# Six PSUM banks for the first propagation of batch 0, and a reordered start, in a two-layer graph kernel

## The reference

```python
h = relu(layernorm(x))                       # (8, 1024, 256)
Xw = h @ Wv + bv;  sj = Xw @ aw[:d];  si = Xw @ aw[d:]
e = leaky_relu(sj[:, None, :] + si[:, :, None] + ab, 0.2)
T = adj * exp(e);  T = T / (T.sum(-1) + 1e-12)
H = h @ Wk[0] + T @ (h @ Wk[1]) + T @ T @ (h @ Wk[2]) + bk.sum(0)   # as the kernel groups it
x = x + relu(H)
h = relu(layernorm(x));  A1 = adj + I;  dh = rsqrt(A1.sum(-1))
x = x + relu(dh * (A1 @ (dh * h)) @ kernel + bias)
```

## Time and profile before

| | us |
|---|---|
| median of 3 runs | 764.09 |
| the runs | 763.99, 764.09, 766.89 |
| profiled execution | 765.5 |
| its span (first to last instruction) | 763.7 |
| PE busy, share of the span | 749.1, 98% |
| DVE busy | 623.8, 82% |
| ACT busy | 536.9, 70% |
| POOL busy | 187.1, 24% |
| moved by DMA | 143.32 MB, mean 188 GB/s |

### The profile page before, as it was taken

The page is one execution under the profiler, slowest core; times in us unless marked ns, Lnnn a source line. Parts: engine busy times, 40 slices in busy tenths (PEclk is TensorE's granted clock), DMA queues, the critical chain, the costliest instruction groups (busy, mean ns, idle before and its releaser), DMA issues.

```text
span 763.7 us, 14034 instructions
## 1 busy us (share of the span) xinstructions
PE 749.1 (98%) x5099; PEld 689.8 (90%) x5099; DVE 623.8 (82%) x1417; ACT 536.9 (70%) x1044; POOL 187.1 (24%) x190
## 2 busy tenths in 40 slices
PE   8879999999999999999999999999999999999997
PEld 8778998999889898998979999899998999889986
DVE  7877888978888789887998879897888877986665
ACT  3887796667966689557885678856696677956451
POOL 3023141222403224041321304122140222402330
PEclk9989999999999999999999999999999999999999
DMA  6557348753486445872657625776248654455511
GB/s 223 211 183 251 115 163 277 224 203 129 156 284 210 174 153 172 284 248 85 194 186 266 231 77 189 241 258 223 95 155 275 214 208 139 156 184 183 168 64 55
DMA packets 63909, 143.32 MB, mean 188 GB/s; under 512 B 6768, under 2 KB 32864, under 8 KB 63840
## 3 DMA queue, kind: packets, MB, share of 16 engines
q1 hardware_dynamic: 55072, 111.75, 43.9%
q10 hardware_dynamic: 8768, 30.68, 11.4%
HBM read 133.96 MB, written 8.45 MB: 186 GB/s over the span
## 4 chain that ended last, share of the span: by engine, by line
PE 94%; DVE 3%; ACT 1%; issue 1%; DMA 0%; POOL 0%; POOLq 0%; DVEq 0%; ACTq 0%
PE acc L1176 15%; PE acc L1178 15%; PE acc L1177 15%; PE da L1044 14%; PE db L1044 8%; PE da L1142 4%; PE tp L1142 4%; PE da L1144 4%; PE da L1143 4%; PE tp L1144 4%; PE tp L1143 4%; PE acc L1076 1%; PE acc L1195 1%; DVE t_raw L806 1%; PE acc L1197 1%
## 5 line engine op out<-in xcount | busy, mean ns | idle before, releaser
L1176 PE MATMUL acc<-g_hi,t_hi 128*128 128x256 f32 (+1 forms) x976 | 276.6, 283 | 0.1
L1178 PE MATMUL acc<-g_hi,t_lo 128*128 128x256 f32 (+1 forms) x976 | 275.2, 282 | 0.0
L1177 PE MATMUL acc<-g_lo,t_hi 128*128 128x256 f32 x976 | 274.6, 281 | 0.0
L1177 PEld LDWEIGHTS acc<-g_lo,t_hi 128*128 128x128 f32 x976 | 184.3, 189 | 0.4
L1176 PEld LDWEIGHTS acc<-g_hi,t_hi 128*128 128x128 f32 x976 | 183.8, 188 | 0.9 <-DVE g_lo L780 0.3
L1178 PEld LDWEIGHTS acc<-g_hi,t_lo 128*128 128x128 f32 x976 | 184.1, 189 | 0.0
L398 POOL TENSOR_TENSOR g_lo<-tmp,g_hi 128x256 fp32r<-128x256 f32 x64 | 61.9, 967 | 266.4 <-ACT g_hi L578 266.4
L817 DVE TENSOR_TENSOR a_lo<-a_raw,a_hi 128x512 fp32r<-128x512 f32 x128 | 94.1, 750 | 23.9 <-ACT a_hi L566 23.8
L523 ACT ACTIVATE tg_e<-si,sij 128x256 f32<-128x256 f32 x256 | 109.5, 501 | 0.1
L566 ACT CAST a_hi<-a_raw 128x512 fp32r<-128x512 f32 x128 | 76.8, 618 | 26.0 <-DVE a_raw L856 17.9
L404 POOL TENSOR_TENSOR hs_lo<-tmp,hs_hi 128x256 fp32r<-128x256 f32 x64 | 60.0, 957 | 89.7 <-ACT hs_hi L463 89.7
(11 more groups left out here) (153 smaller groups left out, 1615.4 us busy)
## 6 DMA issues: line engine op xcount, KB each, us to landing
a_raw<-adj_dram SPq DMA_DIRECT2D x64, 512.0 KB, 4.4
a_raw<-adj_z_dram SPq DMA_DIRECT2D x64, 512.0 KB, 4.3
tg_a<-adj_t_dram ACTq DMA_DIRECT2D x58, 512.0 KB, 4.3
x_o<-x_dram SPq DMA_DIRECT2D x64, 128.0 KB, 3.5
out_dram<-x_o SPq DMA_DIRECT2D x64, 128.0 KB, 4.0
x_nat<-x_dram SPq DMA_DIRECT2D x28, 256.0 KB, 4.9
xt<-x_t_dram SPq DMA_DIRECT2D x28, 256.0 KB, 5.4
si<-mean_rows_dram SPq DMA_DIRECT2D x7, 512.0 KB, 4.6
```

Of the source, the lines that this page charges most:

```text
L1176: nc.tensor.matmul(acc[:, s, 0:n], l_hi, r_hi, start=(jt == 0), stop=False)
L1177: nc.tensor.matmul(acc[:, s, 0:D], l_hi, r_lo, start=False, stop=False)
L1178: ins = nc.tensor.matmul(acc[:, s, 0:n], l_lo, r_hi, start=False, stop=(jt == NT - 1))
```

## The change

- `WARM` goes from (24, 16, 10) to (24, 4, 14).
- `norm0(0)` and `norm0(1)` move ahead of the second half's `moments`, from behind the `v` columns.
- `bk_sum` is summed by GpSimd, after its two powers and ahead of the low parts of the weights; VectorE waits for it (`bk_ready`) ahead of `first_p0`.
- `first_lo(3)` moves ahead of `bk_sum`'s wait and of the first `first_p0`.
- `mean_copy(1)` moves behind `leaky(0, 6)` on ScalarE.
- Batch 0's U phase uses six banks, the three of `acc`, then `db`, `da` 0 and `da` 1 (`first_acc`); the wait for a bank is for tile i-6. The turn of the mean moves from ahead of the second halves of tiles 2 and 3 to between them. The dense products of batch 1, which write `da` and `db`, wait for `u_chunk(5)`.

```diff
-    WARM = (24, 16, 10)
+    WARM = (24, 4, 14)
...
+        FB = AB + OB
+        def first_acc(i):
+            return [acc[:, s] for s in range(AB)][i % FB] if i % FB < AB else out_bank[i % FB - AB]
...
             for h in range(2):
                 power(rstd0, ve0, ve_first, h + 1, rstd_first, slice(h * HJ, (h + 1) * HJ))
+            pool.wait_ge(loaded_w, 16 * 4)
+            nc.gpsimd.tensor_tensor(bk_sum[:, :], bk_raw[:, 0, :], bk_raw[:, 1, :], ALU.add).then_inc(bk_ready, 1)
+            pool.wait_ge(bk_ready, 1)
+            nc.gpsimd.tensor_tensor(bk_sum[:, :], bk_sum[:, :], bk_raw[:, 2, :], ALU.add).then_inc(bk_ready, 1)
...
             for u in range(HJ, NU - 1):
+                leaky(0, u)
                 if u == NU - 2:
                     mean_copy(1)
-                leaky(0, u)
                 exponent(0, u)
...
                 ins.then_inc(stats_first, 1)
+                if h == 1:
+                    dve.wait_ge(rstd_first, 1)
+                    norm0(0)
+                    norm0(1)
                 moments(h + 1, st0, mv0, ve0, stats_first, mean_first, ve_first, range(h * HJ, (h + 1) * HJ))
...
             ins.then_inc(v_cols_ready, 1)
-            dve.wait_ge(rstd_first, 1)
-            norm0(0)
-            norm0(1)
...
             first_sij(3)
-            dve.wait_ge(loaded_w, 16 * 4)
-            then(nc.vector.tensor_tensor(bk_sum[:, :], bk_raw[:, 0, :], bk_raw[:, 1, :], ALU.add))
-            then(nc.vector.tensor_tensor(bk_sum[:, :], bk_sum[:, :], bk_raw[:, 2, :], ALU.add))
+            first_lo(3)
+            dve.wait_ge(bk_ready, 2)
             first_p0(FIRST_P0[0])
-            first_lo(3)
...
                 if b > 1:
                     pe.wait_ge(z_tmp_done, (b - 1) * NT)
+                else:
+                    pe.wait_ge(g1_tmp_ready, FB)
...
-            def accumulate_halves(b, cp, middle):
+            def accumulate_halves(cp, middle):
                 for jh in range(2):
-                    pe.wait_ge(t_ready, b * NU + 2 * cp + jh + 1)
-                    if jh == 1 and middle is not None:
-                        middle()
+                    pe.wait_ge(t_ready, 2 * cp + jh + 1)
                     for i in (2 * cp, 2 * cp + 1):
-                        s = acc_slot(U_PHASE, i)
-                        if jh == 0 and i >= AB:
-                            pe.wait_ge(g1_tmp_ready, b * NT + i - AB + 1)
-                        elif jh == 0 and b > 0:
-                            pe.wait_ge(v_tmp_done, b * NT + i - AB + 1)
+                        if jh == 1 and i % 2 and middle is not None:
+                            middle()
+                        s = first_acc(i)
+                        if jh == 0 and i >= FB:
+                            pe.wait_ge(g1_tmp_ready, i - FB + 1)
```

More of the change, by code:

```diff
@@ L176, in gnn_two_layers @@
         v_cols_ready = sem("v_cols_ready")
+        bk_ready = sem("bk_ready")
         sij0_ready = sem("sij0_ready")
@@ L820, in u_chunk @@
             def u_chunk(b, i):
-                s, a = i % 2, acc_slot(U_PHASE, i)
+                s = i % 2
+                ps = first_acc(i) if b == 0 else acc[:, acc_slot(U_PHASE, i)]
                 dve.wait_ge(acc_full, b * PHASES + i + 1)
-                nc.vector.tensor_scalar_add(row_t[:, i:i + 1], acc[:, a, D:D + 1], EPS_ROW).then_inc(row_t_done, 1)
+                nc.vector.tensor_scalar_add(row_t[:, i:i + 1], ps[:, D:D + 1], EPS_ROW).then_inc(row_t_done, 1)
                 dve.wait_ge(row_t_done, b * NT + i + 1)
@@ L830, in u_chunk @@
                     dve.wait_ge(g1_ready, b * NT + i - 1)
-                nc.vector.scalar_tensor_tensor(out=tmp[:, s, :], in0=acc[:, a, 0:D], scalar=rinv[:, i:i + 1],
+                nc.vector.scalar_tensor_tensor(out=tmp[:, s, :], in0=ps[:, 0:D], scalar=rinv[:, i:i + 1],
                                                in1=p1[:, i, :], op0=ALU.mult, op1=ALU.add).then_inc(g1_tmp_ready, 1)
@@ L1179, in accumulate @@
                 ins.then_inc(acc_full, 1)
-            def accumulate_halves(b, cp, middle):
+            def accumulate_halves(cp, middle):
                 for jh in range(2):
-                    pe.wait_ge(t_ready, b * NU + 2 * cp + jh + 1)
-                    if jh == 1 and middle is not None:
-                        middle()
+                    pe.wait_ge(t_ready, 2 * cp + jh + 1)
                     for i in (2 * cp, 2 * cp + 1):
-                        s = acc_slot(U_PHASE, i)
-                        if jh == 0 and i >= AB:
-                            pe.wait_ge(g1_tmp_ready, b * NT + i - AB + 1)
-                        elif jh == 0 and b > 0:
-                            pe.wait_ge(v_tmp_done, b * NT + i - AB + 1)
+                        if jh == 1 and i % 2 and middle is not None:
[3 more added lines that the diff above has]
+                            pe.wait_ge(g1_tmp_ready, i - FB + 1)
                         for jt in range(jh * HJ, (jh + 1) * HJ):
                             l_hi, l_lo = t_hi[:, i, jt, :], t_lo[:, i, jt, :]
-                            nc.tensor.matmul(acc[:, s, 0:D + 2], l_hi, g2_hi[:, jt, :], start=(jt == 0), stop=False)
-                            nc.tensor.matmul(acc[:, s, 0:D], l_hi, g2_lo[:, jt, :], start=False, stop=False)
-                            ins = nc.tensor.matmul(acc[:, s, 0:D + 2], l_lo, g2_hi[:, jt, :], start=False, stop=(jt == NT - 1))
+                            nc.tensor.matmul(s[:, 0:D + 2], l_hi, g2_hi[:, jt, :], start=(jt == 0), stop=False)
+                            nc.tensor.matmul(s[:, 0:D], l_hi, g2_lo[:, jt, :], start=False, stop=False)
+                            ins = nc.tensor.matmul(s[:, 0:D + 2], l_lo, g2_hi[:, jt, :], start=False, stop=(jt == NT - 1))
                         if jh == 1:
@@ L1208, in batch @@
                         if i % 2 == 0:
-                            accumulate_halves(b, i // 2, (lambda: rows_of_mean(b + 1)) if b == 0 and i == 2 else None)
+                            accumulate_halves(i // 2, (lambda: rows_of_mean(1)) if i == 2 else None)
                         continue
```

## The result

| | before | after |
|---|---|---|
| median of 8 runs each, us | 763.73 | 759.88 |
| lowest and highest | 762.69, 766.89 | 758.46, 761.27 |
| profiled execution, its span | 765.5, 763.7 | 760.17, 758.4 |

The ratio of after to before is 0.9946, with a 95% interval of 0.9928 to 0.9963. The gain is 3.9 us where 7.25 was forecast: the sign and the place were right, the size was off by nearly half.

A forecast was written before the change was run, and what follows sets the result against it. TensorE, 94% of the chain, bounds the kernel, so only its standing or slow time can be won: 6.3 us in the first propagation plus 0.95 at the start, 764.09 - 7.25 = 756.8 us, range 755.2 to 760.2.

The forecast's parts named there:

- my own bounds: Whole kernel: 755.9 to 758.0 us, from 0.5 and 1.2 for the start and about 0.7 either way for the units.
- the start: Start of batch 0, before the first propagation: reordered norms, fewer warm transposes and the moved bias sum save 0.95 us.
- The new stalls: TensorE waits for units 4, 5 and 6 and before batch 1's dense products: 1.24, 0.18, 0.22 and 1.4 us.
- rival 3: First propagation: T's supply or row sums run later than summed and replace the bank waits; 759.3 to 761 us; chance 0.08.
- the term of 8.5 us: First propagation of batch 0: TensorE's loss before, 5.3 us standing for banks plus 3.2 us slow clock, all removed.
- 6.3: First propagation to batch 1's dense start: net gain in us, 8.5 - 1.24 - 0.18 - 0.22 - 0.55.
- the free case: Start of batch 0: VectorE is not slowed by GpSimd, and the start gains 1.2 us.
- the poor end: Start of batch 0: VectorE's norms and small adds contend with GpSimd, and the start gives only 0.5 us.
- 1: New stalls: TensorE's clock falls, each fall costing about 1.6 us; one gives 758.4, two 760.0 us; chance 0.17.
- 2: First propagation: unit 5's transfer does not move with the start, whose gain is lost; 757.8 us; chance 0.08.
- 4: First propagation: fewer warm transposes and new stalls leave TensorE at half clock; slower, up to 775 us; chance 0.03.
- 5: First propagation: the stall goes but nothing is gained, since another engine bound the work behind it; chance 0.03.

The follow-up runs named there:

- after again: The changed kernel run once more, unchanged, for a second look at its start: 760.46 us, ratio to before 0.9941.
- start alone: The kernel before with only the start's changes (warm transposes, norms, bias sum on GpSimd, earlier first_lo(3)), still three banks: 763.85 us, ratio to before 1.0001.
- quiet splits: The changed kernel with GpSimd's g1_lo of tiles 0 and 1 held until t_low of units 5 and 6 is done: 760.84 us, ratio to before 0.9945.
- mean copy first: The changed kernel with mean_copy ahead of leaky(0, 6) on ScalarE again: 761.17 us, ratio to before 0.9954.
- banks alone: The kernel before with only the six banks, the mean's turn and the mean_copy move: 759.84 us, ratio to before 0.9944.
- xt late: The changed kernel with GpSimd's bias sum waiting for all eight norms, and batch 1's xt transfers issued two units later on SyncE: 759.14 us, ratio to before 0.9932.
- bias on VectorE: The changed kernel with the bias sum back on VectorE, behind first_lo(3) and in front of first_p0: 760.40 us, ratio to before 0.9954.
- dense early: xt late with batch 1's centred_hi(0) and centred_lo(0) one chunk sooner: 759.41 us, ratio to before 0.9932.
- chunks late: dense early with u_chunk(0) to (3) moved behind t_prod and t_low on VectorE: 759.78 us, ratio to before 0.9937.

## Why the prediction was right and where it was not

*The forecast's mechanism was right, its size was not.* No wait for `tmp`, three for `t_lo` instead, the clock full in the stage, and 0.2 us of new waiting behind the dense start; the banks carry the whole gain. That 759.88 lies inside the range is in part luck. It is 0.3 below the upper end, past my own bounds of 755.9 to 758.0, in the room that I had kept for a falling clock and a late transfer. The traced execution of after had neither in the stage. Two terms too large filled that room: of the 3.4 us between 7.25 and 3.85, 0.95 is the start, 1.4 the slow clock of the one execution, 0.5 the stage's new waits and 0.2 the rest; 0.4 is the median of before itself (764.09 of three runs, 763.73 of eight).

*The new stalls* were sized nearly right in sum. Counted as the prediction counts, from the last product's start plus 0.12 (idle + 0.28 - 0.12), they are 1.00, 0.63, 0.59 and 1.01, 3.2 together, against 1.24, 0.18, 0.22 and 1.4, 3.0. Units 5 and 6 came later than summed because `t_low` took 1.76 beside GpSimd, 1.69 to the next step instead of 1.14, the "contention in each chunk" of rival 3. The first is shorter because unit 5's transfer, 0.46 late in the earlier trace rows, was in time here and VectorE ran 0.3 ahead of my sum. The last is shorter only because TensorE arrived later: counted from the start of the stage the dense products began after 27.03, where I had 61.4 - 34.87 = 26.5. ScalarE's queue sets that point: it began `centred_hi(0)` at 60.73, 25.5 behind the start of the stage, where the sum has 25.0. Part of the 0.5 is that it had to wait for VectorE, which the slow `t_low` had delayed. From the timeline of ScalarE in after:

```profile
53.64 1.05 ACT L547 CAST t_hi<-t_raw 128x1024 fp32r<-128x1024 f32 x1 [0.49 <-DVE t_raw L816]
```

*The step that failed in the banks' part* is the term of 8.5 us that is lost before, and its use against the median. It is true of the one execution (32.79 - 27.03 = 5.76 was gained in the pair, against 6.3), but its 3.2 us of slow clock are not the usual price. Two other executions that came to the same two stalls took 31.49 and 31.38. With 31.4 as the usual time, which is an estimate from these two and fits the clocks of the 51 runs, the term is 7.1, and the sum 4.9 by my own stalls, 4.4 by the measured stage. I had written that the execution lay 1.4 above the median, and then took the whole 7.25 off the median, as if the excess were part of both. It was largely the very thing that the change removes.

*The step that failed in the start* is "nearer the free case, since `first_lo` reads PSUM". That was true of `first_lo`, but it was not the instruction that mattered: the norms (0.73 to 1.43, and 1.74 in after again) and both small adds (0.16 to 0.69) stand in front of it. The whole of it, 1.75 us in after, is more than the 0.7 between my two bounds, so even the poor end, 0.5, was too good. Four executions with the changed start (after, after again, start alone, quiet splits) began the first propagation at 35.19 to 35.38, at the late end of the 34.55 to 35.40 of the start of before; only in mean copy first, with its late transfer, did it begin sooner. Start alone against before has 1.0001 in the medians: the term is nothing. The bound should have come from the row of 0.70 in the earlier trace rows applied to each instruction in the stretch, not to one of them. Free of contention it was worth about 1.4 (33.38 to 33.88 against 34.55 to 35.40), so the sum of the free case was sound.

*The rivals.* 1 and 2 were seen once, in after again, and cost 0.9 together; the cause of the second was not the one I gave, since the start was in its place. 3 holds for `t_low`, with 0.4 us for each of two units. 4 did not happen in the propagation, but its premise failed: TensorE was not fed without a gap from 6.9 to 12 us, and in after the clock was low from 9.6 to 13.0, at no cost. 5 is refuted by banks alone.

*A better version.* Quiet start, after with one wait on GpSimd, has the lowest median, 758.90 us, and is 0.9934 (0.9917 to 0.995) of before. That it beats after is likely from the traces and the nine ratios above, but not settled by its own interval. xt late adds a shorter stage in its trace and nothing that its median can show.

*Left open.* What decides in a single execution whether the clock falls, after a stall of 1.7 to 2.8 us or, once, in the start; how much of the excess of 765.5 lies outside the stage; why unit 5's transfer was 1.09 late in after again and 0.40 in quiet start; and how much the move of `mean_copy` is worth.

## What to carry to other kernels

Before a stall is priced from one profile, ask how far that execution lies above the median, and whether the excess sits in the stall: if it does, take it off the price, since the change can't win in the median what the median never lost. An engine that looks free (GpSimd at 24%) is not a free place for work if the instructions of the relieved engine slow down beside it, as VectorE's did; look at which VectorE instructions, of all in that stretch, the moved work will lie beside, and hold it back until they are through. A slowed instruction costs only where the next step waits for it: the norms of 1.64 us in bias on VectorE held next to nothing up. After the bank waits were gone, four attempts at shifting work among the engines (mean copy first, quiet splits, dense early, chunks late) mostly moved the wait. That the next gain has to take work out of the engine that sets the pace is my conclusion from them; no run here tests it.

## What the runs showed of the hardware

- VectorE beside a GpSimd instruction on SBUF: two 128x256 normalisations took 1.43 to 1.76 us instead of 0.73 (1.16 where GpSimd began part of the way through); a 128x1 add of two SBUF operands 0.65 to 0.71 instead of 0.16, as long as the GpSimd instruction beside it (0.72); a 128x1024 subtraction 1.76 instead of 1.22, while GpSimd's 128x256 one took 1.32 instead of 0.74. A 128x512 subtraction with one operand in PSUM took 0.67 to 0.69 in either case.
- TensorE's clock: after 2.71 us of standing it stayed at 2.4 GHz in one execution, after 2.80, 2.73, 2.28, 2.23 and 1.72 us it went to 1.2 GHz, for 3 to 6 us. From 14 us on, no stall of up to 1.55 us (the dense wait of quiet splits) was followed by the lower level. In the start a short stall is no surety: in after the clock fell about 0.7 us behind one of 0.48, in xt late it stayed full behind one of 1.24.
- A slow stretch ahead of a stall partly hides in it (2.23 us of standing became 0.93), so the two prices don't add up.
